# Making the next layer's projection weights and rotary tables within a layer's last round, with the remainders on GpSimd

## The chip, the cores and the metric

The kernel runs on one core of a Trainium2 chip. The metric is the device time of one execution in microseconds, lower is better. Engines are named as the profile names them: PE (TensorE), PEld (its weight loads), DVE (VectorE), ACT (ScalarE), POOL (GpSimd) and SP (SyncE, which here only issues DMAs).

## The reference

The input is 16 sequences of 256 tokens with 128 channels. A first block (linear attention with a running state) is followed by a second block of six layers. Each layer is local attention with rotary tables and then a feed-forward, on all 16 sequences:

```python
def attn_layer(x, Wqkv, qs, ksc, Wo):
    qkv = x @ Wqkv                               # 128 -> 3 * 1024
    q, k, v = jnp.split(qkv, 3, -1)
    q, k, v = (sh(q), sh(k), sh(v))              # 16 heads of 64
    q = l2norm(q) * qs
    k = l2norm(k) * ksc
    q = q * cos * scale + rotate_half(q) * sin * scale
    k = k * cos * inv + rotate_half(k) * sin * inv
    out = local_attention(q, k, v)               # windows of 32, looking one window back
    return out @ Wo
...
for i in range(DEPTH):                           # DEPTH = 6
    x = attn_layer(shift_tokens(x), Wqkv[i], q_scale[i], k_scale[i], Wo[i]) + x
    x = ffn_layer(shift_tokens(x), ln_g[i], ln_b[i], W1[i], b1[i], W2[i], b2[i]) + x
```

All inputs are float32. The kernel does the projection `x @ Wqkv` as a sum of three products of a rounded high part and a remainder: hi·hi, hi·lo and lo·hi.

## The kernel before

After the first block (about 280 us) the six layers run as one software pipeline of **rounds**. A round takes one sequence (a batch of 256 tokens) into the pipeline and works at the same time on the three batches ahead of it, so 96 batches make 99 rounds. Each batch passes four stages, one a round: stage A (projection, squares for the norm, rotary), B (transposes, attention), C (output projection, layer norm), D (feed-forward). Batches of the next layer follow those of the layer before without a break: the first round of a layer has stage A of the new layer and stages B, C and D of the old.

The order of the work on each engine is written out by hand in the table `ORDER`, one row of words for each engine, and `run_slots` walks it once a round. A word is a step and its number; the number of apostrophes is the lag, that is how many rounds ago its batch entered (none is stage A, one is B, two are C, three are D). All engines run in order and wait for each other through counted semaphores. For POOL the row is

```python
    "pool": """
        norm.6' add.0 add.1 add.2 norm.7' add.3 add.4 norm.0 add.5 norm.1 norm.2 add.6 norm.3 norm.4 add.7
        norm.5 """,
```

and for PE it begins

```python
    "pe": """
        proj.0 proj.1 tr.2' pt.3'' w1.1''' tr.3' ot.1'' pv.3'' proj.2 proj.3 tr.4' w1.2''' ot.2'' tr.5'
        proj.4 ot.3'' tr.6' w2.0''' tr.7' proj.5 proj.6 qk.0' wo.0'' qk.1' proj.7 v.0 mean.0'' pt.0' qk.2'
```

The steps that matter here:

- `proj.c` and `v.i`: the 12 pieces of the projection. On PE three 512-column matmuls each (L631 to L633 for `proj`, L646 to L648 for `v`), on ACT the square of the result (L853) or its copy (L860), on DVE the products with the rotary tables (L1176, L1177).
- `add.c` and `norm.c` on POOL (L972, L978): the sum of the two rotary products, and its scaling by the inverse norm, which DVE makes in ten small instructions (`rsqrt.0`, L1206 to L1225). `tr.c'` on PE (L655) transposes the scaled piece.
- `mk.u'` on ACT (L877) writes the mask into the score bank, and `qk.u'` on PE (L668) adds the scores to it.
- `xs.0` on ACT and DVE: the high part and remainder of the activations. `w2.0'''` on DVE (L1279) makes a batch's result, once a round.

**At a layer's edge** the new weights have to be split. The raw weights `wqkv_raw` of the next layer are loaded by SP in the third round after an edge, so they are there long before they are used. They have 3072 columns, in three thirds of 1024: queries, keys, values. `conv_a` runs between the last round of a layer and the first of the next: on ACT it waits until all 12 pieces of the last batch are projected and rounds the first third (`w_a`, L797); on DVE it makes the four rotary tables `rots` with the new scales (L1054, L1055) and then the remainder of the first third (`w_a`, L1066). Thirds two and three follow as `wa.1` and `wa.2`, right behind `xs.0`. On PE, `proj.0` waits for the first remainder (`w_lo` at 3·layer+1), `proj.2` for the second and `v.0` for the third. There are five such edges. The weights of layer 0 are made before the rounds begin.

Of the kernel before, what the change touches and what calls it, by code (L numbers as in the profile page):

```python
# [21 lines left out]
F32 = mybir.dt.float32  # L22
# [6 lines left out]
P = 128  # L29
NB, T, D = 16, 256, 128  # L30
NT = T // P
# [24 lines left out]
    "act": """  # L56
        xs.0 wa.1 wa.2 tr.0' qk.3'' w1.0''' tr.1' ot.0'' proj.0 proj.1 tr.2' pt.3'' w1.1''' ot.1'' tr.3'
# [40 lines left out]
def build(nc, x_in, w_in, w_out_in, Wqkv, q_scale, k_scale, Wo, ln_g, ln_b, W1, b1, W2, b2,  # L98
          rotary, masks, ident_in, pick_in, gather_in, seg_in, out):
    ctx = ExitStack()  # L100
    with ctx:
# [194 lines left out]

        def pipeline(eng, body, conv_a=None, loads=None):
# [26 lines left out]

        def run_slots(steps, engine, n, g, lags, layer, c_layers, conv_c=None, end=0):


            for kind, i, lag in order(engine):
                step = steps.get(kind)
                if step is None:  # L330
                    continue
                if kind == "wa":

                    if layer is not None and not is_first(layer):
                        step(layer, i)
                    continue
                if kind == "wc":

                    if conv_c is not None and conv_c[0] == lag:
                        step(n - lag, conv_c[1], i)  # L340
                    continue
                if kind == "rsqrt":

                    if 0 in lags or 2 in lags:
                        step(n, 0 in lags, 2 in lags)
                elif lag in lags:
                    if kind in ("proj", "v"):
# [46 lines left out]
        W_DMAS = 20  # L394
        W_THIRD = INNER


        @block.sync
        def _(sp):
# [79 lines left out]

            def body(n, g, lags, layer, c_layers, conv_c=None, end=0):  # L480
                has_a, has_b, has_c, has_d = (lag in lags for lag in (0, 1, 2, 3))
# [303 lines left out]
        def _(act):  # L785
            act.wait_ge(start, 1)

            def conv_a(layer):

                act.wait_ge(w_in_sem, (layer + 1) * (W_DMAS * 16))  # L790
                act.wait_ge(proj_full.sem, proj_full.at(layer * NB, 12))
                w_a(layer, 0)

            def w_a(layer, k):

                cols = slice(k * W_THIRD, (k + 1) * W_THIRD)
                act.activation(wqkv_hi[:, cols], wqkv_raw[:, cols], ACT.Copy).then_inc(w_hi, 1)  # L797

            def row_norm(first):
# [3 lines left out]
                if not first:  # L803
                    conv_a(0)
                    w_a(0, 1)
                    w_a(0, 2)
                for k in range(8):
# [141 lines left out]
            for k in range(4):  # L949
                w_cs(0, 0, k)  # L950
            steps.update({"wa": w_a, "wc": w_cs})
            pipeline(act, lambda *z, **k: run_slots(steps, "act", *z, **k), conv_a)


        @block.gpsimd
        def _(pool):
# [24 lines left out]

            steps = {"add": a_add, "norm": a_norm}
            pool.wait_ge(x1_saved, 16)
# [4 lines left out]
        def _(dve):  # L988
# [58 lines left out]
            def conv_a(layer):  # L1047

                dve.wait_ge(w_in_sem, (layer + 1) * (W_DMAS * 16))
                dve.wait_ge(roped.sem, roped.at(layer * NB, 8))  # L1050
                for kind in range(2):
                    sc = qks_raw[:, kind, :]
                    sw = sc.rearrange("p (a d) -> p a d", a=2)[:, ::-1, :].unsqueeze(1).broadcast_to([P, NT, 2, DH // 2])
                    dve.tensor_tensor(rots[:, :, 2 * kind, :], rot[:, :, 2 * kind, :], sc.unsqueeze(1).broadcast_to([P, NT, DH]), ALU.mult)  # L1054
                    dve.tensor_tensor(rots[:, :, 2 * kind + 1, :].rearrange("p t (a d) -> p t a d", a=2),  # L1055
                                      rot[:, :, 2 * kind + 1, :].rearrange("p t (a d) -> p t a d", a=2), sw, ALU.mult)
                w_a(layer, 0)

                dve.wait_ge(w_lo, 3 * layer + 1)

            def w_a(layer, k):

                cols = slice(k * W_THIRD, (k + 1) * W_THIRD)
                dve.wait_ge(w_hi, 3 * layer + k + 1)
                dve.wait_ge(proj_full.sem, proj_full.at(layer * NB, 12))
                dve.tensor_tensor(wqkv_lo[:, cols], wqkv_raw[:, cols], wqkv_hi[:, cols].bitcast(F32), ALU.subtract).then_inc(w_lo, 1)  # L1066
# [6 lines left out]
            conv_a(0)  # L1073
            w_a(0, 1)
            w_a(0, 2)
            dve.wait_ge(la_wc, 1)
# [207 lines left out]

            steps["wa"] = w_a
            def fin_add_(k):
# [5 lines left out]

            steps["fin"] = fin_add_
            pipeline(dve, lambda *z, **k: run_slots(steps, "dve", *z, **k), conv_a)
            fin_add_(7)

# [59 lines left out]
```

## Time and profile before

| | |
|---|---|
| Time, median of 3 runs | 3593.33 us (3586.91 to 3593.59) |
| Time of the profiled execution | 3582.8 us |
| Its span, first to last instruction | 3579.8 us |
| Busy: PE, DVE | 3386.0 us (95%), 3116.5 us (87%) |
| Busy: ACT, POOL | 2507.2 us (70%), 1846.9 us (52%) |
| Mean granted TensorE clock | 0.981 of full speed |

The profiled execution lies 10.5 us below the median of the runs shown, and 4.1 us below the fastest of them. The span is cut into rounds by an instruction that occurs once in each, such as L1279 on DVE. A row of a timeline gives the start, the duration from the first start to the last end of what the row merges, the engine, the line, the operation and its tiles, how many instructions it merges, and in brackets the idle time of the engine before it with what ended it.

### The profile page before, as it was taken

To read this page: it belongs to the slowest core of one execution; us is meant where nothing else is said; L and a number is where in the kernel's file an instruction comes from. 1 tells how busy PE (TensorE), PEld (TensorE's weight loads), DVE (VectorE), ACT (ScalarE), POOL (GpSimd) and SP (SyncE) were. 2 spreads that over 40 slices of the span, in tenths; PEclk is the share of its full clock that TensorE was granted. 3 is DMA by queue.
4 is the path that set the end of the run, shared out by engine and by line. 5 is a ranking of instruction groups with operands and counts; after the bars stand their busy time and mean duration, and the time that the engine had idled before them with its cause. 6 is when DMAs were issued, how large, how long until landed. Compare 5 with 4: busy or idle time off the path is not lost.

```text
span 3579.8 us, 150019 instructions
## 1 busy us (share of the span) xinstructions
PE 3386.0 (95%) x63524; PEld 2724.3 (76%) x63524; DVE 3116.5 (87%) x6016; ACT 2507.2 (70%) x4543; POOL 1846.9 (52%) x1604
## 2 busy tenths in 40 slices
PE   5767999999999999999999999999999999999997
PEld 2325888877888887788887888887788887888885
DVE  8987888888888888888888888888888889888884
ACT  2015777777777777777777777777777777777774
POOL 1434555655555555456555455555565564555561
PEclk9988999999999999999999999999999999999999
DMA  2002433333333333433232433332432332333333
GB/s 85 12 27 53 95 76 83 73 66 78 91 83 79 69 75 74 95 83 75 65 83 59 110 79 71 73 81 58 113 76 63 83 79 61 81 72 70 83 78 82
DMA packets 186825, 267.79 MB, mean 75 GB/s; under 512 B 31670, under 2 KB 89908, under 8 KB 185396
## 3 DMA queue, kind: packets, MB, share of 16 engines
q1 hardware_dynamic: 186164, 258.24, 32.0%
q8 instruction: 505, 8.27, 1.0%
q14 instruction: 156, 1.28, 0.1%
HBM read 22.30 MB, written 4.19 MB: 7 GB/s over the span
## 4 chain that ended last, share of the span: by engine, by line
PE 86%; issue 7%; DVE 4%; ACT 1%; POOL 1%; SPq 1%; DMA 0%; DVEq 0%; POOLq 0%; ACTq 0%
PE bank L668 10%; PE bank L655 10%; PE bank L720 9%; PE obank L702 8%; PE bank L753 7%; PE bank L631 7%; PE bank L633 5%; PE bank L632 5%; PE bank L678 5%; PE bank L712 4%; PE bank L646 3%; PE bank L760 3%; PE bank L648 2%; PE bank L647 2%; PE bank L740 2%
## 5 line engine op out<-in xcount | busy, mean ns | idle before, releaser
L978 POOL TENSOR_TENSOR qn<-qn,rinv 128x512 f32<-128x512 f32 x768 | 796.5, 1053 | 1310.0 <-DVE rinv L1225 1310.0
L972 POOL TENSOR_TENSOR qn<-ropec,ropes 128x512 f32<-128x512 f32 x768 | 990.5, 1304 | 203.4 <-DVE ropes L1177 156.2
L853 ACT ACTIVATE sq<-bank 128x512 f32<-128x512 f32 x768 | 456.2, 599 | 151.8 <-PE bank L633 107.9
L1176 DVE TENSOR_TENSOR ropec<-bank,rots 128x512 f32<-128x512 f32 x768 | 523.7, 682 | 17.2 <-ACT sq L853 10.3
L1185 DVE TENSOR_REDUCE ss<-sq 128x8 f32<-128x512 f32 x768 | 496.8, 676 | 41.8 <-ACT sq L853 41.8
L1177 DVE TENSOR_TENSOR ropes<-bank,rots 128x512 f32<-128x512 f32 x768 | 521.8, 679 | 0.0
L655 PE MATMUL bank<-ident,qn 128*128 128x128 f32 x3072 | 469.7, 276 | 19.2 <-ACT qT L871 11.8
L668 PE MATMUL bank<-kT,qT 64*32 64x64 f32 x24576 | 430.9, 217 | 18.4 <-issue 13.5
L668 PEld LDWEIGHTS bank<-kT,qT 64*32 64x32 f32 x24576 | 368.1, 107 | 102.0 <-issue 80.2
L655 PEld LDWEIGHTS bank<-ident,qn 128*128 128x128 f32 x3072 | 368.1, 141 | 87.9 <-POOL qn L978 27.8
L631 PE MATMUL bank<-wqkv_hi,xs_hi 128*128 128x512 f32 x768 | 363.5, 473 | 27.3 <-issue 18.6
L877 ACT ACTIVATE bank<-mask_f 128x512 f32<-128x512 f32 x384 | 231.7, 603 | 188.8 <-DVE Pr L1236 185.8
L720 PE MATMUL bank<-OT,wo 128*128 128x256 f32 x1536 | 357.2, 385 | 0.7 <-DVE x L1279 0.7
L702 PE MATMUL obank<-V,PT 64*32 64x65 f32 x24576 | 334.2, 225 | 7.6 <-issue 7.5
L702 PEld LDWEIGHTS obank<-V,PT 64*32 64x32 f32 x24576 | 269.5, 105 | 73.6 <-issue 73.5
L860 ACT ACTIVATE Vt<-bank 128x512 f32<-128x512 f32 x384 | 225.1, 586 | 141.9 <-PE bank L648 141.8
L720 PEld LDWEIGHTS bank<-OT,wo 128*128 128x128 f32 x1536 | 283.9, 190 | 44.5 <-issue 1.0
L753 PE MATMUL bank<-xn,w 128*128 128x256 f32 (+1 forms) x1152 | 310.2, 392 | 2.2 <-DVE hm L1273 2.2
L1231 DVE TENSOR_REDUCE mx<-bank 128x8 f32<-128x512 f32 x384 | 263.8, 687 | 55.0 <-PE bank L668 55.0
L633 PE MATMUL bank<-wqkv_hi,xs_lo 128*128 128x512 f32 x768 | 307.4, 400 | 0.0
L632 PE MATMUL bank<-wqkv_lo,xs_hi 128*128 128x512 f32 x768 | 306.1, 399 | 0.0
L871 ACT ACTIVATE kT<-bank 128x512 f32<-128x512 f32 x384 | 229.4, 597 | 73.4 <-PE bank L655 67.6
(138 smaller groups left out, 6275.6 us busy)
## 6 DMA issues: line engine op xcount, KB each, us to landing
V<-Vt SPq DMA_DIRECT2D x576, 260.0 KB, 4.5
V<-Vt SPq DMA_DIRECT2D x192, 130.0 KB, 4.6
V<-Vt SPq DMA_DIRECT2D x192, 65.0 KB, 4.1
xres<-X SPq DMA_DIRECT2D x96, 128.0 KB, 2.1
X<-x SPq DMA_DIRECT2D x96, 128.0 KB, 2.1
wqkv_raw<-L_ffn_Wqkv SPq DMA_DIRECT2D x6, 1536.0 KB
xraw<-X SPq DMA_DIRECT2D x97, 64.0 KB
xraw<-X SPq DMA_DIRECT2D x97, 63.8 KB
```

What stands on the lines that cost most here:

```text
L631: pe.matmul(o, xs_hi[:, rows], wqkv_hi[:, cols], start=True, stop=False)
L633: pe.matmul(o, xs_lo[:, rows], wqkv_hi[:, cols], start=False, stop=True).then_inc(proj_full.sem, 1)
L655: mm = pe.transpose(b_trA[:, j * P:(j + 1) * P], qn[:, c, j * P:(j + 1) * P], ident[:])
L668: mm = pe.matmul(b_sim[w * WIN:(w + 1) * WIN, col:col + 2 * WIN], qT[64 * par:64 * par + 64, m, q0:q0 + WIN], kT[64 * par:64 * par + 64, m ...
L702: mm = pe.matmul(obank[w * WIN:(w + 1) * WIN, slot, j * 65:j * 65 + 65], PT[rows, u % 2, j * P + w * WIN:j * P + (w + 1) * WIN], V[rows, w ...
L720: mm = pe.matmul(b_c[:, 0:T], wo[:, i, :], OT[:, i, :], start=i == 0, stop=i == 7)
L753: mm = pe.matmul(b_c[0:n, part * T:(part + 1) * T], w1[:, cols], xn[:], start=True, stop=True)
L972: pool.tensor_tensor(qn[:, c, :], ropec[:, c % ROPE_RING, :], ropes[:, c % ROPE_RING, :], ALU.add).then_inc(rope_sum.sem, 1)
L978: pool.tensor_tensor(heads8(qn[:, c, :]), heads8(qn[:, c, :]), rinv[:, 8 * c:8 * c + 8].unsqueeze(2).broadcast_to([P, 8, DH]), ALU.mult).t ...
L1176: dve.tensor_tensor(halves(ropec[:, c % ROPE_RING, :]), raw, table(t, 2 * kind), ALU.mult)
L1177: dve.tensor_tensor(halves(ropes[:, c % ROPE_RING, :]), raw[:, :, ::-1, :], table(t, 2 * kind + 1), ALU.mult).then_inc(roped.sem, 1)
L1185: dve.tensor_reduce(ss[:, 8 * c:8 * c + 8], heads8(sq[:, c % 2, :]), AX.X, ALU.add).then_inc(ss_done.sem, 1)
```

## The change

`conv_a` goes out of the pipeline's edge, and `wa.1` and `wa.2` out of the tables. Steps named `third` stand within the rounds now, by a small table `EDGE` of the step that they follow:

- ACT rounds the first third behind `proj.7` and the second behind `v.1` of the last round of a layer, and the last third behind `proj.1` of the first round of the next. Each waits for the last projection of the old batch that reads that third (6, 8 or 12 pieces), not always for all 12.
- POOL, not DVE, makes the rotary tables and the first remainder behind `add.4` of the last round, the second remainder behind `norm.5` of it, and the third behind `add.2` of the first round. Before the tables it waits for all 8 rotary products of the old batch.
- DVE has none of this work but in layer 0, and waits for `rots_done` before `proj.0` of a new layer.
- PE's instructions and waits are as before.

```diff
-        xs.0 wa.1 wa.2 pv.2'' w1.0''' sums.0 sums.1 proj.0 proj.1 w1.1''' pv.3'' proj.2 w1.2''' sums.2
+        xs.0 pv.2'' w1.0''' sums.0 sums.1 proj.0 proj.1 w1.1''' pv.3'' proj.2 w1.2''' sums.2
...
+        EDGE = {"act": {"last": {("proj", 7): 0, ("v", 1): 1}, "first": {("proj", 1): 2}},
+                "pool": {"last": {("add", 4): 0, ("norm", 5): 1}, "first": {("add", 2): 2}}}
...
                 for g in range(3, NB):
-                    body(l * NB + g + 1, g, (0, 1, 2, 3), None, {2: l, 3: l})
-                conv_a and conv_a(l + 1)
-                body(l * NB + NB + 1, 0, (0, 1, 2, 3), l + 1, {2: l, 3: l})
+                    body(l * NB + g + 1, g, (0, 1, 2, 3), None, {2: l, 3: l},
+                         edge=("last", l + 1) if g == NB - 1 else None)
+                body(l * NB + NB + 1, 0, (0, 1, 2, 3), l + 1, {2: l, 3: l}, edge=("first", l + 1))
...
+                if edge is not None and lag == 0 and engine in EDGE:
+                    third = EDGE[engine][edge[0]].get((kind, i))
+                    if third is not None:
+                        steps["third"](edge[1], third)
...
+        THIRD_READ = [1 + max(PROJ_ORDER.index(("proj", c)) for c in range(8) if chunk(c)[0] == kind) for kind in range(2)] + [12]
...
-            def conv_a(layer):
+            def w_a(layer, k):
 
                 act.wait_ge(w_in_sem, (layer + 1) * (W_DMAS * 16))
-                act.wait_ge(proj_full.sem, proj_full.at(layer * NB, 12))
-                w_a(layer, 0)
-
-            def w_a(layer, k):
-
+                act.wait_ge(proj_full.sem, proj_full.at(layer * NB, THIRD_READ[k]))
                 cols = slice(k * W_THIRD, (k + 1) * W_THIRD)
                 act.activation(wqkv_hi[:, cols], wqkv_raw[:, cols], ACT.Copy).then_inc(w_hi, 1)
...
+            def w_a(layer, k):
+
+                if k == 0:
+                    pool.wait_ge(roped.sem, roped.at(layer * NB, 8))
+                    rotary_scaled(pool).then_inc(rots_done, 1)
+                cols = slice(k * W_THIRD, (k + 1) * W_THIRD)
+                pool.wait_ge(w_hi, 3 * layer + k + 1)
+                pool.tensor_tensor(wqkv_lo[:, cols], wqkv_raw[:, cols], wqkv_hi[:, cols].bitcast(F32), ALU.subtract).then_inc(w_lo, 1)
...
+                if c == 0 and layer is not None and not is_first(layer):
+                    dve.wait_ge(rots_done, layer)
```

On POOL, from `add.3` and `add.4` of the last round of the first layer to `add.0` to `add.2` of the next round, there stood before (L972 is `add`, L978 `norm`):

```order
L972 TENSOR_TENSOR qn<-ropec,ropes 128x512 x2
L978 TENSOR_TENSOR qn<-qn,rinv 128x512
L972 TENSOR_TENSOR qn<-ropec,ropes 128x512
L978 TENSOR_TENSOR qn<-qn,rinv 128x512 x2
L972 TENSOR_TENSOR qn<-ropec,ropes 128x512
L978 TENSOR_TENSOR qn<-qn,rinv 128x512 x2
L972 TENSOR_TENSOR qn<-ropec,ropes 128x512
L978 TENSOR_TENSOR qn<-qn,rinv 128x512 x2
L972 TENSOR_TENSOR qn<-ropec,ropes 128x512 x3
L978 TENSOR_TENSOR qn<-qn,rinv 128x512
```

and now, with L981 for `add`, L987 for `norm`, first the part around `add.4` in the last round:

```order
L981 TENSOR_TENSOR qn<-ropec,ropes 128x512 x2
L386 TENSOR_TENSOR rots<-rot,qks_raw 128x2x64
L387 TENSOR_TENSOR rots<-rot,qks_raw 128x2x64
L386 TENSOR_TENSOR rots<-rot,qks_raw 128x2x64
L387 TENSOR_TENSOR rots<-rot,qks_raw 128x2x64
L998 TENSOR_TENSOR wqkv_lo<-wqkv_raw,wqkv_hi 128x1024
L987 TENSOR_TENSOR qn<-qn,rinv 128x512
```

and then the part from `add.7` and `norm.5` to `norm.7'` of the next round:

```order
L981 TENSOR_TENSOR qn<-ropec,ropes 128x512
L987 TENSOR_TENSOR qn<-qn,rinv 128x512
L998 TENSOR_TENSOR wqkv_lo<-wqkv_raw,wqkv_hi 128x1024
L987 TENSOR_TENSOR qn<-qn,rinv 128x512
L981 TENSOR_TENSOR qn<-ropec,ropes 128x512 x3
L998 TENSOR_TENSOR wqkv_lo<-wqkv_raw,wqkv_hi 128x1024
L987 TENSOR_TENSOR qn<-qn,rinv 128x512
```

Five instructions stand ahead of `norm.0` that were not there, one stands between `norm.5` and `norm.6'`, and one between `add.2` and `norm.7'`.

On ACT, in the same last round, from `proj.7` (L853, then L862) to `mk.3'` (the second L877, then L886), there stood before:

```order
L853 ACTIVATE sq<-bank 128x512
L877 ACTIVATE bank<-mask_f 128x512
L860 ACTIVATE Vt<-bank 128x8x64
L906 ACTIVATE dsq<-dlt 128x256
L882 ACTIVATE Pr<-Pr 128x512
L888 ACTIVATE PT<-bank 128x512
L860 ACTIVATE Vt<-bank 128x8x64
L877 ACTIVATE bank<-mask_f 128x512
```

and now:

```order
L862 ACTIVATE sq<-bank 128x512
L807 ACTIVATE wqkv_hi<-wqkv_raw 128x1024
L886 ACTIVATE bank<-mask_f 128x512
L869 ACTIVATE Vt<-bank 128x8x64
L915 ACTIVATE dsq<-dlt 128x256
L891 ACTIVATE Pr<-Pr 128x512
L897 ACTIVATE PT<-bank 128x512
L869 ACTIVATE Vt<-bank 128x8x64
L807 ACTIVATE wqkv_hi<-wqkv_raw 128x1024
L886 ACTIVATE bank<-mask_f 128x512
```

A rounding of 1024 columns stands ahead of each of the masks `mk.2'` and `mk.3'`.

## Rows read from the trace of the kernel before

**Rows 1.** The page: busy time by engine; chain that ended last, by engine.

```profile
PE 3386.0 (95%) x63524; PEld 2724.3 (76%) x63524; DVE 3116.5 (87%) x6016; ACT 2507.2 (70%) x4543; POOL 1846.9 (52%) x1604
...
PE 86%; issue 7%; DVE 4%; ACT 1%; POOL 1%; SPq 1%; DMA 0%; DVEq 0%; POOLq 0%; ACTq 0%
```

**Rows 2.** Timeline of DVE: L1279, once a round, around edges 2, 1, 5.

```profile
1288.75 0.47 DVE L1279 SCALAR_TENSOR_TENSOR x<-bank,vec,x 128x256 f32<-128x256 f32 x1
...
1321.83 0.47 DVE L1279 SCALAR_TENSOR_TENSOR x<-bank,vec,x 128x256 f32<-128x256 f32 x1
...
1363.72 0.47 DVE L1279 SCALAR_TENSOR_TENSOR x<-bank,vec,x 128x256 f32<-128x256 f32 x1
...
781.96 0.47 DVE L1279 SCALAR_TENSOR_TENSOR x<-bank,vec,x 128x256 f32<-128x256 f32 x1
...
824.73 0.47 DVE L1279 SCALAR_TENSOR_TENSOR x<-bank,vec,x 128x256 f32<-128x256 f32 x1
...
2948.07 0.47 DVE L1279 SCALAR_TENSOR_TENSOR x<-bank,vec,x 128x256 f32<-128x256 f32 x1
...
2989.33 0.47 DVE L1279 SCALAR_TENSOR_TENSOR x<-bank,vec,x 128x256 f32<-128x256 f32 x1
```

**Rows 3.** Busy time in stretches: a steady one, edge 2, its slow part (columns first).

```profile
core 0: us, PE busy (x) PEld busy (x) DVE busy (x) ACT busy (x) POOL busy (x), PEclk, DMA share, GB/s
1300.00:1332.95 32.95, 32.95 (x657) 27.14 (x656) 29.27 (x59) 25.25 (x47) 18.21 (x16) 1.00 0.34 75
1332.95:1374.85 41.90, 36.29 (x658) 29.58 (x657) 38.94 (x67) 28.61 (x50) 19.44 (x16) 0.88 0.27 60
1344.00:1354.30 10.30, 6.73 (x70) 5.46 (x50) 10.23 (x12) 4.64 (x8) 5.12 (x4) 0.50 0.01 2
```

**Rows 4.** Timeline of PE: a hole at edge 1; `tr.1'` and `proj.0` at edge 2.

```profile
797.21 0.52 PE L668 MATMUL bank<-kT,qT 64*32 64x64 f32 x19 [1.16 <-issue]
797.66 0.61 PE L646 MATMUL bank<-wqkv_hi,xs_hi 128*128 128x512 f32 x1
...
1343.12 0.63 PE L655 MATMUL bank<-ident,qn 128*128 128x128 f32 x4 [2.04 <-ACT qT L871]
1343.68 1.07 PE L702 MATMUL obank<-V,PT 64*32 64x65 f32 x64
1348.32 0.77 PE L631 MATMUL bank<-wqkv_hi,xs_hi 128*128 128x512 f32 x1 [3.57 <-issue]
```

**Rows 5.** What waits for the remainders (L1066): durations, all 18.

```profile
L1066 DVE TENSOR_TENSOR wqkv_lo<-wqkv_raw,wqkv_hi x18: 1210/1641/2284, 32.6 to 2976.4; 128x1024 fp32r<-128x1024 f32 x18
...
  PEld bank L631: 18.3, 5
```

**Rows 6.** Lines of POOL, and the rounding on ACT: durations, min/median/max.

```profile
L972 POOL TENSOR_TENSOR qn<-ropec,ropes x768: 1261/1287/1521, 286.7 to 3510.4; 128x512 f32<-128x512 f32 x192
...
L978 POOL TENSOR_TENSOR qn<-qn,rinv x768: 1033/1044/2021, 303.5 to 3513.7; 128x512 f32<-128x512 f32 x192
...
L797 ACT ACTIVATE wqkv_hi<-wqkv_raw x18: 1039/1044/1056, 29.7 to 2967.7; 128x1024 fp32r<-128x1024 f32 x18
```

**Rows 7.** Timeline of ACT and PE, last round before edge 2: `proj.7`, masks, `qk.2'`.

```profile
1329.59 0.60 ACT L853 ACTIVATE sq<-bank 128x512 f32<-128x512 f32 x1 [0.55 <-PE bank L633]
1330.21 0.60 ACT L877 ACTIVATE bank<-mask_f 128x512 f32<-128x512 f32 x1
...
1333.79 0.60 ACT L877 ACTIVATE bank<-mask_f 128x512 f32<-128x512 f32 x1
...
1331.05 1.10 PE L668 MATMUL bank<-kT,qT 64*32 64x64 f32 x64
```

**Rows 8.** Timeline of DVE and POOL there: `proj.7`, end of `rsqrt`, `norm.0`.

```profile
1330.83 0.68 DVE L1177 TENSOR_TENSOR ropes<-bank,rots 128x512 f32<-128x512 f32 x1
...
1336.73 0.23 DVE L1225 SCALAR_TENSOR_TENSOR rinv<-bank,rinv 128x66 f32<-128x66 f32 x1
...
1337.04 1.04 POOL L978 TENSOR_TENSOR qn<-qn,rinv 128x512 f32<-128x512 f32 x1 [13.72 <-DVE rinv L1225]
```

**Rows 9.** Timeline of POOL: `norm.5` and `norm.6'`, `add.0` to `add.2`, `norm.7'`.

```profile
1312.96 2.04 POOL L978 TENSOR_TENSOR qn<-qn,rinv 128x512 f32<-128x512 f32 x2
1314.96 3.77 POOL L972 TENSOR_TENSOR qn<-ropec,ropes 128x512 f32<-128x512 f32 x3
1318.70 1.03 POOL L978 TENSOR_TENSOR qn<-qn,rinv 128x512 f32<-128x512 f32 x1
```

**Rows 10.** Timeline of PE in the same round: `proj.2`, and `tr.7'`.

```profile
1314.25 0.50 PE L631 MATMUL bank<-wqkv_hi,xs_hi 128*128 128x512 f32 x1
...
1320.78 0.60 PE L655 MATMUL bank<-ident,qn 128*128 128x128 f32 x4
```

More of the change, by code:

```diff
@@ L56 @@
     "act": """
-        xs.0 wa.1 wa.2 tr.0' qk.3'' w1.0''' tr.1' ot.0'' proj.0 proj.1 tr.2' pt.3'' w1.1''' ot.1'' tr.3'
+        xs.0 tr.0' qk.3'' w1.0''' tr.1' ot.0'' proj.0 proj.1 tr.2' pt.3'' w1.1''' ot.1'' tr.3'
         mk.0' proj.2 tr.4' proj.3 w1.2''' wc.2''' ot.2'' tr.5' proj.4 tr.6' ot.3'' tr.7' proj.5 proj.6 mk.1'
@@ L202, in build @@
         const_in = sem("const_in")
+        rots_done = sem("rots_done")
         sim_begun = sem("sim_begun")
@@ L293, in la_pipeline, with pipeline @@
             channels(LA_STEPS, 0, [], True)
-        def pipeline(eng, body, conv_a=None, loads=None):
+        def pipeline(eng, body, loads=None):
             body(1, 0, (0,), 0, None)
@@ L323, in build, with run_slots @@
                      "dve": {"x1": (0, 1), "mean": (2, 3), "rsqrt": (4,), "ln": (5, 6)}}
-        def run_slots(steps, engine, n, g, lags, layer, c_layers, conv_c=None, end=0):
+        EDGE = {"act": {"last": {("proj", 7): 0, ("v", 1): 1}, "first": {("proj", 1): 2}},
+                "pool": {"last": {("add", 4): 0, ("norm", 5): 1}, "first": {("add", 2): 2}}}
+        def run_slots(steps, engine, n, g, lags, layer, c_layers, conv_c=None, end=0, edge=None):
             for kind, i, lag in order(engine):
@@ L330, in run_slots @@
                 if step is None:
[L331 to L335, printed above, removed]
                     continue
@@ L376, in build, with rotary_scaled @@
         UNIT = [(u // 2, u % 2) for u in range(4)]
+        def rotary_scaled(eng):
+            for kind in range(2):
+                sc = qks_raw[:, kind, :]
+                sw = sc.rearrange("p (a d) -> p a d", a=2)[:, ::-1, :].unsqueeze(1).broadcast_to([P, NT, 2, DH // 2])
+                ins = eng.tensor_tensor(rots[:, :, 2 * kind, :], rot[:, :, 2 * kind, :], sc.unsqueeze(1).broadcast_to([P, NT, DH]), ALU.mult)
+                ins = eng.tensor_tensor(rots[:, :, 2 * kind + 1, :].rearrange("p t (a d) -> p t a d", a=2),
+                                        rot[:, :, 2 * kind + 1, :].rearrange("p t (a d) -> p t a d", a=2), sw, ALU.mult)
+            return ins
         def hold(eng, held, s, value):
@@ L478, in place_v, with body @@
                     move(half, 0, 0, P - WIN, slice(1, 2), WIN)
-            def body(n, g, lags, layer, c_layers, conv_c=None, end=0):
+            def body(n, g, lags, layer, c_layers, conv_c=None, end=0, edge=None):
                 has_a, has_b, has_c, has_d = (lag in lags for lag in (0, 1, 2, 3))
@@ L803, in row_norm @@
                 if not first:
-                    conv_a(0)
-                    w_a(0, 1)
-                    w_a(0, 2)
+                    for k in range(3):
+                        w_a(0, k)
                 for k in range(8):
@@ L950, in _ @@
                 w_cs(0, 0, k)
-            steps.update({"wa": w_a, "wc": w_cs})
-            pipeline(act, lambda *z, **k: run_slots(steps, "act", *z, **k), conv_a)
+            steps.update({"third": w_a, "wc": w_cs})
+            pipeline(act, lambda *z, **k: run_slots(steps, "act", *z, **k))
         @block.gpsimd
@@ L980, in a_norm @@
                                    ALU.mult).then_inc(normed.sem, 1)
-            steps = {"add": a_add, "norm": a_norm}
+            def w_a(layer, k):
[5 more added lines that the diff above has]
+                pool.tensor_tensor(wqkv_lo[:, cols], wqkv_raw[:, cols], wqkv_hi[:, cols].bitcast(F32), ALU.subtract).then_inc(w_lo, 1)
+            steps = {"third": w_a, "add": a_add, "norm": a_norm}
             pool.wait_ge(x1_saved, 16)
@@ L1050, in conv_a @@
                 dve.wait_ge(roped.sem, roped.at(layer * NB, 8))
[L1051 to L1059, printed above, removed]
+                rotary_scaled(dve)
             def w_a(layer, k):
@@ L1064, in w_a @@
                 dve.wait_ge(w_hi, 3 * layer + k + 1)
-                dve.wait_ge(proj_full.sem, proj_full.at(layer * NB, 12))
                 dve.tensor_tensor(wqkv_lo[:, cols], wqkv_raw[:, cols], wqkv_hi[:, cols].bitcast(F32), ALU.subtract).then_inc(w_lo, 1)
@@ L1073, in _ @@
             conv_a(0)
-            w_a(0, 1)
-            w_a(0, 2)
+            for k in range(3):
+                w_a(0, k)
             dve.wait_ge(la_wc, 1)
@@ L1283, in _ @@
                      "var": c_var_, "ln": c_ln_, "w1": c_w1, "w2": c_w2}
-            steps["wa"] = w_a
             def fin_add_(k):
@@ L1293, in _ @@
             steps["fin"] = fin_add_
-            pipeline(dve, lambda *z, **k: run_slots(steps, "dve", *z, **k), conv_a)
+            pipeline(dve, lambda *z, **k: run_slots(steps, "dve", *z, **k))
             fin_add_(7)
```

## The prediction

> **What bounds the kernel now.** I read the page first. PE is busy 95% of the span and makes up 86% of the chain that ended last [rows 1], so only what lets PE idle, or slows its clock, counts. Next I cut the span into rounds by L1279. A steady round is 32.95 us long, and in one PE is busy for all 32.95 us at full clock [rows 3]; DVE is at 29.3 us there, so it too has little room. The round that holds edge 2 takes 1363.72 − 1321.83 = 41.89 us. Edge 1 takes 42.77 us and edge 5 takes 41.26 us [rows 2]; edges 3 and 4 are like edge 2, within 0.1 us. The rounds just before and behind an edge are steady to within a microsecond or so, and the change does not touch what makes those differ. So an edge costs PE some 8.9 us, and there are five.
>
> The timeline of PE splits the 8.9 us. Ahead of `tr.1'` PE idles 2.04 us for ACT, whose copy of `tr.0'` stands behind three roundings of 1.04 us. Ahead of `proj.0` it idles 3.57 us for the first remainder, which DVE reaches only after four tables and a 2.28 us subtraction [rows 4, 5]. What is left is 41.89 − 32.95 − 2.04 − 3.57 = 3.3 us: from 1344.0 to 1354.3 the granted clock is 0.50, the lower of the two levels, 1.2 GHz [rows 3]. Two holes in PE's work were enough to bring it down.
>
> **What goes.** Both holes have their cause in `conv_a`, `wa.1` and `wa.2`, and these are taken out from in front of `tr.0'`, `xs.0` and `proj.0`. With them go 8.94 us at edge 2, as much at edges 3 and 4 to within 0.1 us, and 8.3 us at edge 5. Edge 1 has 9.8 us, but its round also has a hole of 1.16 us that the profile lays to "issue", with slower matmuls behind it [rows 4]; I leave 2.7 us of it standing and take 7.1 us. Together: 7.1 + 3 × 8.9 + 8.3 = **42.1 us** at most.
>
> **What comes, on ACT.** The first rounding (1.04 us [rows 6]) stands ahead of `mk.2'`. Now `proj.7` ends at 1330.19, the mask is written from 1330.21 to 1330.81, and PE starts `qk.2'` at 1331.05 [rows 7]. Slack is 0.24 us less what the semaphore takes. With the rounding in between the mask ends at about 1331.8, and PE starts about **0.75 us** late. The second rounding stands ahead of `mk.3'`, now written from 1333.79. With both it ends near 1335.9, where PE, already 0.75 us late, wants it at about the same time; I give it 0.1 us. ACT has spare time behind that, and all later copies of the round stay ahead of their readers. The third rounding, in the next round, delays the copy of `tr.2'` by 1 us and PE by some 0.6 us, but that lies inside the wait for `proj.2` below and adds nothing. The end of `rsqrt`, and POOL with it, moves by 0.7 us too, since DVE waits for `qk.2'`.
>
> **What comes, on POOL.** The four tables and the first remainder have a hole to fill. POOL idles 13.72 us ahead of `norm.0`; of that the stretch from the end of DVE's `proj.7` (1331.51) to the end of `rsqrt` (1336.96, later by 0.7 us) can be used, 6.1 us [rows 8]. The tables are 128 columns each. No row has POOL on such a form; it is between a quarter of L978 and the whole of it, so 0.26 to 1.04 us, nearer the first. With a remainder of 2.5 us the work takes 3.5 to 6.7 us. I take 4 us: **nothing**, and 0.6 us at the upper end. Cover gone, each further microsecond would delay `norm.0`, `tr.0` and PE at once.
>
> The price of a remainder on POOL, d, decides the rest. No row shows it. L972 has the same kind of operands, two full tiles in SBUF, at half the width: 1287 ns, so at most 2.57 us for 1024 columns. L978, with one operand broadcast, would give 2 × 1033 = 2.07 us [rows 6]. I take **d = 2.5 us**, near L972. On DVE the same subtraction took 1.21 us with POOL silent and 2.28 us beside it, and POOL's L978 went from 1.03 to 2.02 us [rows 5, 6], so a contended d would be 4.0 us. But what DVE does beside the second and third remainders reads PSUM or one tile of SBUF; its only subtraction of two SBUF tiles, `xs.0`, lies elsewhere. I leave contention to a rival.
>
> The second remainder follows `norm.5`, and PE's `proj.2` waits for it. In a steady round `norm.5` ends at about 1314.00 [rows 9] and PE starts `proj.2` at 1314.25 [rows 10]. The slack is 0.25 us and the work 2.5 us: PE, itself 0.15 us later than POOL, waits about **2.1 us**. In the queue of POOL there now stand behind it `norm.6'`, three adds, the third remainder and `norm.7'`. No add is late for DVE's ring of three buffers, as DVE is itself held by PE. `norm.6'` is needed 3 us later than it comes. But `norm.7'` ends at 1319.73 and PE wants it at 1320.78 [rows 9, 10]: slack 1.05 us. It comes 0.7 + 2 × 2.5 = 5.7 us late, so PE is 4.65 us late in all, **1.7 us** more than at `proj.2`. The third remainder itself is done before that, and `v.0`, which needs it, comes some 9 us later, so it makes no wait of its own. Sum of idle time for each edge: 2d − 0.35 = **4.65 us** (3.8 at d = 2.07, 4.8 at 2.57), where it was 5.6.
>
> **The clock.** The idle time is now in three pieces of 0.8, 2.1 and 1.7 us with work between. Before, two pieces of 2.04 and 3.57 us cost 3.3 us in slow matmuls. If the clock falls behind the piece of 2.1 us for a short stretch, PE reaches `tr.7'` later, but there it would have waited anyway, so it costs next to nothing. If it falls behind the last piece I price it as half of the 3.3 us that the larger holes cost, about 1.7 us; the 2.7 us left standing at edge 1 are such a stretch too, 1.16 + 1.5 us. I take 0.8 us, with 0 and 3.3 us as the ends. For an edge: 4.65 + 0.8 = 5.45 us, for five 27.3 us.
>
> **The sum.** 42.1 − 27.3 = 14.8 us, say **15 us less**. On the profiled execution that is 3582.8 − 15 = 3568 us. That execution is 10.5 us faster than the median of the runs, with the same rounds, so the gain carries over: 3593.3 − 15 = **3578 us**, 0.42% less. Ends: 42.1 − 5 × 3.8 = 23 us less, and 42.1 − 5 × 8.1 = 2 us less. The DVE work that goes brings nothing beyond that, as PE is the bound wherever DVE was free.
>
> The Trainium skill speaks against the move: GPSIMD Engine Reference, "Engine selection", keeps elementwise work on VectorE, and its section on elementwise work gives 4497 ns against 2293 ns for an add of 2048 columns. The trace agrees in kind: 1.29 us for 512 columns on POOL, 1.21 us for 1024 on DVE. An estimate from that page is 2.25 us for 1024 columns on POOL; the sum would then be 4.15 us of idle time, a gain of about 17 us. The same page says that the two engines share their SBUF interfaces when DVE has two SBUF inputs, and the doubled durations in rows 5 and 6 bear that out.
>
> **The rivals.**
> 1. *No new waits.* All of the thirds hide, the gain is the full 42 us, 3551 us. For it: POOL idles 13.7 us a round. Against it: that hole is not where thirds two and three stand; the slacks there are 0.25 and 1.05 us, read directly.
> 2. *The clock gives it back.* Both later holes bring the clock down as before, each edge then costs 4.65 + 3.3 = 7.95 us and the gain is 42.1 − 39.8 = 2 us: 3591 us. For it: holes of 2.04 and 3.57 us did it at every edge. Against it: 2.1 and 1.7 us are smaller and lie 6.5 us of work apart.
> 3. *Slower: POOL pays the contended price.* With d = 4.0 us (twice 2021 ns), at the second and third remainders, each edge has 2 × 4.0 − 0.35 = 7.7 us idle and 1.7 to 3.3 us of slow clock, 47 to 55 us in all against 42.1: 3598 to 3606 us. It decides from d = 3.5 us on, where 2d − 0.35 + 1.7 = 8.4 us. For it: no row shows POOL writing this type at this width. Against it: DVE has no two-tile SBUF work there.
>
> **How the numbers follow.** My forecast 0.70, rival 1 0.04, rival 2 0.19, rival 3 0.07. About 0.2% (7 us) is what a measurement of this kernel can tell from no change. Forecast and rival 1 give faster, but for the 0.05 of the forecast that lies at its slow end; that and rival 2 are the same; rival 3 is mostly slower. Faster 0.69, same 0.24, slower 0.07. The range goes from 3566 (23 us less, and the 4 us by which runs differ) to 3592 (rival 2).
>
> **What the profile of the changed kernel would show.** L1279, which stands between `proj.2` and `tr.7'` in a round, about 32.95 + 0.85 + 2.1 = 35.9 us apart across an edge, not 41.9, and then 1.7 us more than a steady round in the next interval, with the slow clock on top. No wait ahead of `tr.1'` or `proj.0`. Instead PE waits of some 0.8 us at `qk.2'` for ACT's mask, 2.1 us at `proj.2` for POOL's `wqkv_lo`, and 1.7 us at `tr.7'` for POOL's `qn`. The subtraction on POOL at 2.5 us, the tables well under 1 us each, `norm.0` not later than `rsqrt`. A clock near 0.5 in at most one short stretch an edge. I am wrong if d is above 3.5 us, if PE waits for `rots` or `norm.0`, or if `proj.2` does not wait at all.

## The result, and the profile after

| | before | after |
|---|---|---|
| Time, median | 3590.68 us (6 runs, 3583.43 to 3593.59) | 3564.95 us (6 runs, 3555.07 to 3573.13) |
| Span of the profiled execution | 3579.8 us | 3553.3 us |
| Ratio | | 0.9928 (0.9909 to 0.9946) |

The change makes the kernel 0.72% faster. The median lies 25.7 us below that of before, where 15 us were forecast, and 1 us below the low end of the range. The same pair measured again on another chip (run `again` below) gave 19.5 us, ratio 0.9943 (0.9929 to 0.9957), and the two intervals overlap. One run of before on that chip (12631.61 us) and one of `act_only2` (6948.23 us) were in a slow state; the ratios leave them out, and without them the medians below move by 0.2 us at most.

The page after the change, busy time by engine, which answers to [rows 1]:

```profile
PE 3371.8 (95%) x63524; PEld 2712.1 (76%) x63524; DVE 3070.7 (86%) x5981; ACT 2503.4 (70%) x4543; POOL 1882.7 (53%) x1639
```

DVE has 46 us less to do and POOL 36 us more. PE is busy 14 us less with the same instructions, because it runs fewer of them at the low clock.

The once-a-round instruction on DVE, now L1289, across edge 3 of the changed kernel, to be set beside [rows 2]:

```profile
1853.79 0.47 DVE L1289 SCALAR_TENSOR_TENSOR x<-bank,vec,x 128x256 f32<-128x256 f32 x1
...
1889.61 0.47 DVE L1289 SCALAR_TENSOR_TENSOR x<-bank,vec,x 128x256 f32<-128x256 f32 x1
...
1924.30 0.47 DVE L1289 SCALAR_TENSOR_TENSOR x<-bank,vec,x 128x256 f32<-128x256 f32 x1
```

The round with this edge takes 35.82 us, where it took 41.8 us before, and the one behind it 34.7 us, where a steady one takes 32.95. The timeline of PE at edge 2, only the rows ahead of which it idled, against [rows 4]: `qk.2'`, then `tr.3'` and `proj.2` of the new layer's first round, then `tr.7'`.

```profile
1326.65 1.10 PE L682 MATMUL bank<-kT,qT 64*32 64x64 f32 x64 [0.70 <-ACT bank L886]
...
1341.97 0.63 PE L669 MATMUL bank<-ident,qn 128*128 128x128 f32 x4 [0.47 <-ACT kT L880]
...
1344.97 0.50 PE L645 MATMUL bank<-wqkv_hi,xs_hi 128*128 128x512 f32 x1 [1.09 <-POOL wqkv_lo L998]
...
1353.02 0.66 PE L669 MATMUL bank<-ident,qn 128*128 128x128 f32 x4 [1.34 <-POOL qn L987]
```

Nothing idles ahead of `tr.1'` and `proj.0` any more. The four holes stand where the forecast put them, and all edges look alike but for the one ahead of `proj.2`, which is 0.99 to 1.33 us. They sum to 3.6 to 3.9 us an edge. The profile models where a matmul ends, so starts are the safer measure: against a steady round, PE's starts at edge 3 slip by 0.77 us at `qk.2'`, by 0.63 at `tr.3'`, by 1.40 at `proj.2` and by 1.51 at `tr.7'`, 4.3 to 4.4 us in all. The durations of POOL's new instructions, which no row of before could show (minimum, median, maximum in ns):

```profile
L998 POOL TENSOR_TENSOR wqkv_lo<-wqkv_raw,wqkv_hi x15: 2347/2369/2392, 793.7 to 2960.3; 128x1024 fp32r<-128x1024 f32 x15
```
```profile
L386 POOL TENSOR_TENSOR rots<-rot,qks_raw x10: 448/453/458, 792.0 to 2938.0; 128x128 f32<-128x128 f32 x10
```

And the stretch from the last round's L1289 to well behind edge 2, to be read against the 0.50 of [rows 3] (columns as there, the granted clock behind POOL's):

```profile
1316.69:1385.50 68.81, 63.85 (x1299) 52.49 (x1298) 56.33 (x115) 51.49 (x93) 43.64 (x39) 1.00 0.28 63
```

The clock stays at its high level through the edge, and so it does at all five. PE is busy 63.85 us of these 68.81; besides the four holes there is one of 1.34 us behind the edge that the profile lays to "issue".

### The profile page after: what moved, and what is told of

It reads as the page before. It is cut to its first block, busy times and chain, and to the rows that moved or that the text cites. A ratio compares the mean times of both kernels' runs of the same rounds, so it can differ in the third digit from the quotient of the medians.

```text
span 3553.3 us, 150003 instructions
## 1 busy us (share of the span) xinstructions
PE 3371.8 (95%) x63524; PEld 2712.1 (76%) x63524; DVE 3070.7 (86%) x5981; ACT 2503.4 (70%) x4543; POOL 1882.7 (53%) x1639
## 4 chain that ended last, share of the span: by engine, by line
issue 47%; POOL 33%; PE 16%; DVE 2%; SPq 1%; ACT 1%; POOLq 0%; DMA 0%; DVEq 0%; ACTq 0%
POOL qn L981 21%; POOL qn L987 11%; PE bank L682 2%; PE bank L734 2%; PE bank L669 2%; PE obank L716 1%; PE bank L767 1%; PE bank L645 1%; DVE PT L1149 1%; PE bank L692 1%; PE bank L726 1%; PE bank L647 1%; PE bank L646 1%; POOL wqkv_lo L998 1%; PE bank L774 1%
## 5 line engine op out<-in xcount | busy, mean ns | idle before, releaser
L987 POOL TENSOR_TENSOR qn<-qn,rinv 128x512 f32<-128x512 f32 x768 | 790.8, 1045 | 1251.4 <-DVE rinv L1235 1251.4
L981 POOL TENSOR_TENSOR qn<-ropec,ropes 128x512 f32<-128x512 f32 x768 | 989.5, 1303 | 158.4 <-DVE ropes L1187 116.9
L862 ACT ACTIVATE sq<-bank 128x512 f32<-128x512 f32 x768 | 456.4, 599 | 134.6 <-PE bank L647 90.7
L886 ACT ACTIVATE bank<-mask_f 128x512 f32<-128x512 f32 x384 | 231.8, 604 | 189.2 <-DVE Pr L1246 186.1
```

The costliest lines, as they stand in the source:

```text
L862: act.activation(sq[:, c % 2, :], b_proj[n % 2][:], ACT.Square).then_inc(squared.sem, 1)
L981: pool.tensor_tensor(qn[:, c, :], ropec[:, c % ROPE_RING, :], ropes[:, c % ROPE_RING, :], ALU.add).then_inc(rope_sum.sem, 1)
L987: pool.tensor_tensor(heads8(qn[:, c, :]), heads8(qn[:, c, :]), rinv[:, 8 * c:8 * c + 8].unsqueeze(2).broadcast_to([P, 8, DH]), ALU.mult).t ...
```

## The experiments

All figures for the edges below are worked out in one way: the two intervals of the once-a-round instruction at each edge, less two steady ones of 32.95 us, summed over the five edges. The kernel before has 45.7 us by that, the changed kernel 23.2 us.

| Kernel | against before, us (medians) | ratio | edges, us |
|---|---|---|---|
| changed kernel, first time | −25.7 | 0.9928 (0.9909 to 0.9946) | 23.2 |
| `again` | −19.5 | 0.9943 (0.9929 to 0.9957) | 22.7 |
| `act_only` | +23.4 | 1.0063 (1.0039 to 1.0086) | 69.1 |
| `act_only2` | +5.0 | 1.0013 (1.0003 to 1.0023) | 46.8 |
| `tables_only` | −17.7 | 0.9948 (0.9927 to 0.9968) | 26.8 |
| `twice` | −9.7 | 0.9973 (0.9960 to 0.9985) | 35.9 |
| `act_early` | −22.9 | 0.9934 (0.9921 to 0.9947) | 18.5 |
| `dve_rest` | −30.5 | 0.9905 (0.9887 to 0.9924) | 12.9 |
| `in_the_gap` | −38.9 | 0.9894 (0.9878 to 0.9911) | 1.1 |
| `no_split` | −43.5 | 0.9874 (0.9855 to 0.9892) | 2.2 |

`again`, `no_split`, `act_early` and `in_the_gap` ran on one chip, beside the same runs of before (median 3581.68 us), `act_only`, `dve_rest` and `twice` on a second (3586.28 us), the other two on a third (3584.60 us). Small differences between kernels of different chips are therefore read from the edges of the traces. `no_split` computes with wrong weights and serves only as a bound.

### Is the gain at the edges, and how large is it: `again`

> The changed kernel once more, on another chip run, beside the kernel before. Its trace shows 4.4 us left at each of four edges and 5.6 us at one, where the kernel before had 8.4 to 9.8 us: 22 us less at the edges, 20 us without the idle times that both kernels show at odd places. Theory 'the edges are all of it': 20 to 23 us less than before. Rival 'there is more than the edges' (the measured difference of the medians was 25.7 us): 26 us or more less.

19.5 us less, half a microsecond short of the theory, with 22.7 us left at the edges. The gain at the edges, 45.7 − 22.7 = 23.0 us, covers all of it. The 25.7 us of the first measurement are not borne out. Of the difference between its two profiled executions (26.5 us of span) 22.5 us are at the edges. Of the other 4 us, 1.5 are one round: the one ahead of edge 4 took 35.56 us in the kernel before and 34.05 in the changed one. Both have an "issue" hole there, of 1.25 and 1.22 us, but only before did the clock fall behind it. Such holes stand at scattered places in both kernels and differ between executions.

### What is the most there is to have: `no_split`

```diff
-        EDGE = {"act": {"last": {("proj", 7): 0, ("v", 1): 1}, "first": {("proj", 1): 2}},
-                "pool": {"last": {("add", 4): 0, ("norm", 5): 1}, "first": {("add", 2): 2}}}
+        EDGE = {}
...
-                if layer is not None and c in (0, 2):
+                if layer is not None and is_first(layer) and c in (0, 2):
...
-                if layer is not None and i == 0:
+                if layer is not None and is_first(layer) and i == 0:
...
-                if c == 0 and layer is not None and not is_first(layer):
-                    dve.wait_ge(rots_done, layer)
```

> Leaves out the splitting of the projection weights and the rotary tables of layers 1 to 5 (those of layer 0 are used throughout, so the later layers compute with wrong weights), and the waits on it. This is the most that any placing of this work can give. Theory: all of the 42 us that the edges cost before go, 20 to 22 us less than the changed kernel, and the intervals of L1279 across an edge are those of a steady round, 33 us. Rival 'something else at the edges costs time, such as the loads of the weights or the copies for the later stages': some microseconds stay at each edge.

43.5 us less than before; 42.1 us were worked out for it in the prediction. The intervals at the edges are steady ones to within 0.7 us, 2.2 us in all. So nearly the whole loss was the splitting and its waits.

### Whose queue set the end of the edge: `act_only` and `act_only2`

Both put ACT's three roundings into the rounds, as the change does, and leave tables and remainders on DVE at the edge (`conv_a`, `wa.1`, `wa.2`) as before. They differ in the place of the third rounding (only this line of each is shown):

```diff
 # act_only
+        EDGE = {"act": {"last": {("proj", 7): 0, ("v", 1): 1}, "first": {("proj", 1): 2}}}
 # act_only2
+        EDGE = {"act": {"last": {("proj", 7): 0, ("v", 1): 1}, "first": {("xs", 0): 2}}}
```

> Half of the change: the three roundings stand within the rounds as in the changed kernel, but the tables and all remainders stay on DVE at the edge, as before. Theory 'DVE's queue set the end of the edge': the idle time of 2.04 us ahead of tr.1 goes and the one ahead of proj.0 grows by as much, since DVE is not earlier; with the 0.7 us at qk.2 the idle time is 5.6 to 6.4 us an edge, the clock falls as before, and the time is that of the kernel before to within 5 us. Rival 'ACT's three roundings set it': 2 us and more less at each edge, 10 us or more less than before.

23.4 us more, which neither theory had. The idle time ahead of `tr.1'` did move to `proj.0`, where PE now waits 6.02 us, but there is more. The timeline of DVE in `act_only` at edge 2 shows why:

```profile
1353.84 2.06 DVE L1079 TENSOR_TENSOR wqkv_lo<-wqkv_raw,wqkv_hi 128x1024 fp32r<-128x1024 f32 x1
1358.53 1.23 DVE L1079 TENSOR_TENSOR wqkv_lo<-wqkv_raw,wqkv_hi 128x1024 fp32r<-128x1024 f32 x1 [2.63 <-ACT wqkv_hi L811]
```

DVE runs in order and stands in `wa.2` until ACT has rounded the third third, which now comes behind ACT's `proj.1`, and so behind PE's. Behind DVE in the queue stands `w1.0'''`, for which PE waits another 2.4 to 3.2 us. The experiment had put in a wait of its own (DVE for ACT, ACT for PE), so it was repeated without it.

> As act_only, but with the third rounding behind xs.0 of the first round, so that DVE, which still makes the tables and all remainders at the edge, never waits for ACT. In act_only DVE waited 2.6 us for that rounding and the edge cost 13 to 14 us. Theory 'DVE's queue set the end of the edge': the hole ahead of proj.0 is about 5.6 to 6 us in one piece, PE reaches the new layer no earlier than in the kernel before, 0.7 us later for the mask ahead of qk.2; the time is within 5 us of the kernel before. Rival 'ACT's roundings set it': 10 us or more less than before.

5.0 us more than before, as the theory had it. The hole ahead of `tr.1'` is down from 2.04 to 0.15 us, and the one ahead of `proj.0` has taken it over. PE at edge 2 of `act_only2`:

```profile
1344.72 0.63 PE L673 MATMUL bank<-ident,qn 128*128 128x128 f32 x4 [0.15 <-ACT qT L884]
...
1351.83 0.76 PE L649 MATMUL bank<-wqkv_hi,xs_hi 128*128 128x512 f32 x1 [5.69 <-issue]
```

ACT's half of the change alone gains nothing. The hole of 2.04 us for ACT was real and yet free, since DVE was later still.

### DVE's half, or only its cheapest part: `tables_only`

The kernel before, with the four tables alone moved to POOL, behind `add.4`:

```diff
+                if edge is not None and engine == "pool" and (kind, i, lag) == ("add", 4, 0):
+                    steps["tables"](edge)
...
+            def tables(layer):
+                pool.wait_ge(w_in_sem, (layer + 1) * (W_DMAS * 16))
+                pool.wait_ge(roped.sem, roped.at(layer * NB, 8))
+                rotary_scaled(pool).then_inc(rots_done, 1)
...
             def conv_a(layer):
...
-                for kind in range(2):
...
+                if is_first(layer):
+                    rotary_scaled(dve)
```

> The kernel before with one part of the change: only the four rotary tables go to POOL, behind add.4 of the last round; ACT's roundings and DVE's remainders stay at the edge. Theory: DVE is 4.6 us earlier there, so the hole ahead of proj.0 goes, and the one of 2.04 us ahead of tr.1 for ACT stays; DVE's 5.5 us of remainders delay its products and make a new hole of some 2 us: about 4 us of idle time an edge and 0 to 1.7 us of slow clock, 15 to 25 us less than before. Rival 'the remainders alone hold the edge': 10 us less or nothing.

17.7 us less, within what was expected: the four table instructions alone give most of what the whole change gives. PE at edge 2:

```profile
1346.04 0.63 PE L668 MATMUL bank<-ident,qn 128*128 128x128 f32 x4 [2.04 <-ACT qT L884]
...
1351.98 1.13 PE L766 MATMUL bank<-xn,w 128*128 128x256 f32 x4 [2.03 <-DVE hm L1289]
```

`proj.0` follows without a hole, and the remainders on DVE make a new one ahead of `w1.1'''`, of 0.5 to 2.0 us. Where it is only 0.5 or 0.7 us, PE had come to it later, held up by a stretch of low clock; the round with the edge is 4.75 us longer than a steady one either way. That stretch came behind the single hole of 2.04 us at three edges (1, 4 and 5) and not at the other two.

### What a hole costs in clock: `twice`

```diff
+        spare = sb("spare", [P, 1024], F32R)
...
                 pool.wait_ge(w_hi, 3 * layer + k + 1)
+                if k == 1:
+                    pool.tensor_tensor(spare[:], wqkv_raw[:, cols], wqkv_hi[:, cols].bitcast(F32), ALU.subtract)
```

> The changed kernel with the second remainder made twice on POOL (the first time into a spare tile), 2.4 us more between norm.5 and norm.6. Theory 'POOL's queue is what PE waits for, one for one, and longer holes bring the clock down': the wait ahead of proj.2 grows from 1.3 to about 3.7 us and the granted clock falls behind it: 2.4 us more idle time an edge and 0 to 1.7 us of slow clock, 12 to 20 us more than the changed kernel. Rival 'no slow clock below the 5.6 us of idle time of the kernel before': just 12 us more, with no stretch at 0.50 at an edge.

About 10 us more than the changed kernel (−9.7 against −19.5 us, measured on two chips), 12.7 us by the edges; the theory had 12 to 20. PE at edge 2, and the clock behind the hole:

```profile
1350.37 0.80 PE L646 MATMUL bank<-wqkv_hi,xs_hi 128*128 128x512 f32 x1 [3.64 <-POOL wqkv_lo L1001]
```
```profile
1348.80:1355.70 6.90, 5.33 (x15) 3.99 (x16) 1.29 (x2) 1.68 (x3) 6.63 (x6) 0.51 1.04 221
```

The hole has grown from 1.1 or 1.3 us to 3.64, one for one with the 2.37 us put in, and the granted clock falls to its lower level behind it at every edge. But three of the five edges cost just 2.2 to 2.4 us more than in the changed kernel: PE, slower for a while, reaches `tr.7'` when POOL has just finished, and the hole of 1.34 us ahead of it is gone. At the other two the low clock lasted twice as long, 6.8 us, and cost about 0.9 us beyond the hole. This is the case which the prediction priced at next to nothing. Both theories had a part of it: the clock does fall, and it is mostly free here.

### The three waits one by one: `act_early`, `dve_rest`

`act_early` moves the first rounding to where ACT idled:

```diff
-        EDGE = {"act": {"last": {("proj", 7): 0, ("v", 1): 1}, "first": {("proj", 1): 2}},
+        EDGE = {"act": {"last": {("proj", 6): 0, ("v", 1): 1}, "first": {("proj", 1): 2}},
```

> The first rounding on ACT moved from behind proj.7 to behind proj.6 of the last round, where ACT idled 1.9 us. Theory 'the 0.70 us ahead of qk.2 is the first rounding': that wait goes, the later ones stay, 0.7 us less at each edge, 3.5 us less in all than the changed kernel. Rival 'PE only waits for POOL, which is then earlier too, or the second rounding takes its place': under 1 us less in all, or a new wait at qk.3.

3.4 us less than `again` by the medians, 4.2 us by the edges. The intervals of the two kernels overlap, so it is the trace that shows it: the hole of 0.70 us ahead of `qk.2'` is at no edge, the others are unchanged.

`dve_rest` takes the second and third remainder from POOL:

```diff
-                "pool": {"last": {("add", 4): 0, ("norm", 5): 1}, "first": {("add", 2): 2}}}
+                "pool": {"last": {("add", 4): 0}, "first": {}},
+                "dve": {"last": {}, "first": {("xs", 0): 1, ("proj", 1): 2}}}
...
+                if k and not is_first(layer):
+                    dve.wait_ge(w_lo, 3 * layer + k)
```

> The changed kernel, but with remainders two and three on DVE (behind xs.0 and behind proj.1 of the first round) and not on POOL. DVE needs 1.2 us for one alone and up to 2.3 us beside POOL. Theory 'both engines are tight there, DVE more so, since it is busy 29 of 33 us': the waits ahead of proj.2 for wqkv_lo and ahead of tr.7 for POOL go, and PE waits instead some 1.5 us for DVE's rotary products before proj.2 and again behind the second one; within 5 us of the changed kernel. Rival 'GpSimd is simply the slower engine for it': 8 us or more faster than the changed kernel.

30.5 us less than before. The theory falls: DVE was not too tight. The two remainders on DVE at edge 2:

```profile
1342.90 2.29 DVE L1077 TENSOR_TENSOR wqkv_lo<-wqkv_raw,wqkv_hi 128x1024 fp32r<-128x1024 f32 x1
...
1349.92 1.50 DVE L1077 TENSOR_TENSOR wqkv_lo<-wqkv_raw,wqkv_hi 128x1024 fp32r<-128x1024 f32 x1
```

Only the second was clearly faster than POOL's 2.37 us, and PE waited for DVE only 0.24 to 0.41 us at a time. The edges cost 12.9 us, 10 us less than in the changed kernel. With the tables gone, DVE had room for two remainders and POOL had not.

### A version that beats both: `in_the_gap`

```diff
-        EDGE = {"act": {"last": {("proj", 7): 0, ("v", 1): 1}, "first": {("proj", 1): 2}},
-                "pool": {"last": {("add", 4): 0, ("norm", 5): 1}, "first": {("add", 2): 2}}}
+        EDGE = {"act": {"last": {("proj", 6): (0, 1), ("v", 0): (2,)}, "first": {("proj", 6): (3,)}},
+                "pool": {"last": {("add", 4): (0, 1, 2)}, "first": {("add", 4): (3,)}}}
...
+        PIECES = [(0, 1024), (1024, 1536), (1536, 2048), (2048, 3072)]
+        PIECE_READ = [1 + PROJ_ORDER.index(("proj", c)) for c in (5, 6, 7)] + [12]
```

> The same work in four pieces (1024, 512, 512 and 1024 columns), each placed where its engine idles: ACT rounds pieces 0 and 1 behind proj.6, piece 2 behind v.0 of the last round, piece 3 behind proj.6 of the first round; POOL makes remainders 0 and 1 behind add.4 of the last round, ahead of the tables, then tables and remainder 2, and remainder 3 behind add.4 of the first round, in its idle stretch of 13.7 us. Theory 'what is left at an edge is the three waits of PE and nothing else': all three go, 4.3 us less at each edge, 20 to 22 us less than the changed kernel, some 3544 us. Rival 'POOL's share of its idle stretch slows DVE, or ACT has no room for piece 2': 10 us or less of it.

3542.8 us, some 3544 expected; 38.9 us less than before and 19.4 us less than the changed kernel on the same chip; the intervals do not meet. The second third is cut in halves because its first half is last read by `proj.6` and can be rounded in the same idle stretch of ACT. POOL's remainder of the values waits until behind `add.4` of the first round:

```profile
1881.62 2.54 POOL L981 TENSOR_TENSOR qn<-ropec,ropes 128x512 f32<-128x512 f32 x2 [1.06 <-DVE ropes L1187]
1885.44 2.36 POOL L998 TENSOR_TENSOR wqkv_lo<-wqkv_raw,wqkv_hi 128x1024 fp32r<-128x1024 f32 x1 [1.27 <-ACT wqkv_hi L807]
1897.84 1.04 POOL L987 TENSOR_TENSOR qn<-qn,rinv 128x512 f32<-128x512 f32 x1 [10.04 <-DVE rinv L1235]
```

and the rounds across edge 3 are steady ones, 32.94 us:

```profile
1849.72 0.47 DVE L1289 SCALAR_TENSOR_TENSOR x<-bank,vec,x 128x256 f32<-128x256 f32 x1
...
1882.66 0.47 DVE L1289 SCALAR_TENSOR_TENSOR x<-bank,vec,x 128x256 f32<-128x256 f32 x1
...
1915.60 0.47 DVE L1289 SCALAR_TENSOR_TENSOR x<-bank,vec,x 128x256 f32<-128x256 f32 x1
```

The work of splitting is all still there, and its time cannot be told from that of leaving it out (3542.8 against 3538.1 us, with overlapping intervals; 1.1 against 2.2 us at the edges).

## Why the prediction was right and wrong

**What bounds the kernel, and what goes: right, but for edge 1.** 42.1 us were to be had; `no_split` measured 43.5. The prediction counted the 2.04 us for ACT and the 3.57 us for DVE as two gains. They were one, as `act_only2` showed: taking ACT's away only lengthened the wait for DVE. It did no harm, since the change removed both. The 2.7 us left standing at edge 1, for its hole of 1.16 us laid to "issue" and the slow matmuls behind it, did not stand: in the changed kernel that edge has an "issue" hole of 0.32 us in one trace and none in the other, and costs what the others do. What makes such holes come and go stays open. The rounds beside an edge were also less steady than the prediction says: the one ahead of edge 4 took 35.56 us.

**What comes on ACT: right.** 0.75 us at `qk.2'` were forecast, 0.70 came, and `act_early` took just this away. The third rounding's hole (0.6 us forecast, 0.47 measured) lies inside the wait for `proj.2`, as said.

**What comes on POOL: right in place, a little too dear.** The tables and the first remainder are hidden (4.2 us of work; `norm.0` follows `rsqrt`). A remainder takes 2.37 us, not 2.5. With that the prediction's own formula for how late PE is gives 2 × 2.37 − 0.35 = 4.39 us an edge. At seven of the ten edges in the two traces of the changed kernel the two intervals are together 4.31 to 4.36 us longer than steady ones; the other three, up to 5.58 us, have odd idle time behind the edge as well. The first interval was forecast at 35.9 us and is 35.8; the second was to be 1.7 us longer than a steady one, and is 1.4. So the lateness was mis-sized by 0.3 us an edge, 1.5 us in all. The page of the Trainium skill (GPSIMD Engine Reference, "Elementwise") would have done no better: half of its 4497 ns for 2048 columns, an estimate of 2.25 us for 1024, is as far below the 2.37 us as 2.5 is above. Neither scaling by width holds exactly. From 1287 ns at 512 columns and 2369 ns at 1024, POOL's instruction costs an estimated 2.1 ns a column and 0.2 us besides, which doubling the 1287 ns counts twice.

**The clock: the term that failed.** The prediction took 0.8 us an edge, 4 us in all, and gave 0.19 to a case with 3.3 us. It measured 0. In both traces of the changed kernel the granted clock is at its upper level throughout all five edges, behind 30 holes of 0.69 to 1.37 us. The step that failed is "two holes in PE's work were enough to bring it down", carried over to smaller ones. `twice` shows that the low clock comes back with a hole of 3.64 us, and the kernel before had it with 2.04 and 3.57 us together. But the size of a hole does not decide alone: the clock fell behind the single one of 2.04 us in `tables_only` at three edges of five, and in the kernel before it fell behind one of 1.16 us at edge 1 and one of 1.25 us ahead of edge 4. What else decides was not looked into.

**The sum.** 15 us forecast. The clock (4 us), edge 1 (2.7 us) and the lateness (1.5 us) put right, it is 23.2 us; at the edges of the two traces 22.5 and 23.0 us went. So these three terms account for what the forecast missed at the edges, all on the same side. The medians gave 25.7 and 19.5 us, on either side of it.

**The range: wrong by 1 us.** Its low end, 3566 us, holds a gain of 23 us, which is what the edges gave, and 4 us more by which runs differ. It was counted from 3593.3 us, the median of three runs of before. With three runs more that median is 3590.7 us, and the gain of 25.7 us taken from there ends below 3566. Counted from the same median, the measured gain lies inside the 27 us that the range allowed, so it was chance that the time fell outside; that the forecast was 8 us too low at the edges was not. That what goes beyond the edges' 23 us is spread between executions, and not an effect of the change, is made likely by `again` and is not shown.

**The rivals.** Rival 2 is out, since the clock gave nothing back, and rival 3 as well, since a remainder took 2.37 us and not 4.0. Rival 1 (no new waits, 42 us) did not happen, for the reason given. But it was reachable, by the placing of `in_the_gap`: POOL's 13.7 us of idle time, which the prediction named in its favour, hold all remainders.

## What to carry to other kernels

When two engines make the bound wait in turn, find the one whose queue ends last before a price is put on each hole: four small table instructions taken off DVE's queue were worth 17.7 us, three roundings taken off ACT's none while DVE's queue still ended later. Work that is moved "into the round" is not hidden by that; read the slack of its reader at the new place (0.25 and 1.05 us here) and look for the place where both the source is done and the engine idles, cutting a piece in two if one half is free sooner. And a slow stretch of the clock ahead of a wait for another engine costs what it adds beyond that wait, which was nothing at three edges of `twice` and at three of `tables_only`.

## What the hardware showed that was not expected

DVE's small instructions on two tiles of SBUF waited for whole instructions of POOL. DVE and POOL in the kernel before, at edge 2:

```profile
1340.47 0.99 DVE L1054 TENSOR_TENSOR rots<-rot,qks_raw 128x128 f32<-128x128 f32 x1
1341.38 1.35 DVE L1055 TENSOR_TENSOR rots<-rot,qks_raw 128x128 f32<-128x128 f32 x1
1342.66 1.13 DVE L1054 TENSOR_TENSOR rots<-rot,qks_raw 128x128 f32<-128x128 f32 x1
1343.71 1.12 DVE L1055 TENSOR_TENSOR rots<-rot,qks_raw 128x128 f32<-128x128 f32 x1
...
1339.27 2.05 POOL L978 TENSOR_TENSOR qn<-qn,rinv 128x512 f32<-128x512 f32 x2
1341.27 1.32 POOL L972 TENSOR_TENSOR qn<-ropec,ropes 128x512 f32<-128x512 f32 x1
1342.55 2.14 POOL L978 TENSOR_TENSOR qn<-qn,rinv 128x512 f32<-128x512 f32 x2
```

Each table ends 0.14 to 0.15 us after one of POOL's instructions has ended: the first at 1341.46 behind 1341.32, the second at 1342.74 behind 1342.59, the fourth at 1344.83 behind 1344.69. A table of 128 columns on DVE took 0.28 us with POOL silent, and at the edges 0.99 to 1.36 us (once 0.54) beside POOL's norms and adds, which last 1.0 to 1.3 us each. On POOL, in the changed kernel, the same table took 0.45 us. This is why the tables, the smallest part of the work in columns, cost the most at the edge of the kernel before: 4.4 us of DVE's queue for 512 columns in all.

The chain of work that ended last changed its look without a change in the kernel's steady state:

```profile
issue 47%; POOL 33%; PE 16%; DVE 2%; SPq 1%; ACT 1%; POOLq 0%; DMA 0%; DVEq 0%; ACTq 0%
```

Before it was 86% PE [rows 1]. PE is as busy as it was, and `tr.0` starts within 0.1 us of the end of `norm.0` in 77 of 96 rounds, as in 76 of 96 before. It seems that the chain can take either side of such a tie; that this is the reason was not shown. The chain of the changed kernel follows POOL through whole rounds and lays POOL's idle time, 13.64 us a round, to "issue", so its shares alone would have named the wrong bound here.
